# Edge stages of a two-layer graph network: a fixed loop over edge groups, index loads for four groups, row and column tiles on TensorE

## The chip, the core and the metric

The kernel runs as one program on one core of one Trainium2 chip. The metric is the device time of one execution in microseconds (us); lower is better. Engines are called PE (TensorE matmul), PEld (its weight loads), DVE (VectorE), ACT (ScalarE), POOL (GpSimd) and SP (SyncE).

## The reference

There are 12,500 nodes with 128 features and 200,000 edges that are sorted by their destination `dst`. Two message-passing layers run one after the other, each on the layer-normed, clamped nodes, and each is added to the nodes:

```python
# layer 0
h = concat(node[src], node[dst], edge_attr_64) @ W1 + b1
messages = (relu(layernorm(h)) @ W2 + b2) * sigmoid(edge_attr_64 @ gate_w + gate_b)
agg = segment_sum(messages, dst)          # then a GRU cell on agg and the nodes
# layer 1
w = silu(silu(radial(edge_length) @ w0 + b0) @ w1 + b1) @ w2 + b2       # (edges, 4, 32)
m0, m1, m2, m3 = products of w, the sender's features and the edge's direction
out = segment_sum([m0, m3, m1, m2], dst) @ W_out
```

## The kernel before

Edges are worked on in **groups** of 512 (four tiles of 128 edges), 392 groups in all. As the edges are sorted by destination, the destinations of one group nearly always lie in one window of 128 nodes. A group whose destinations spread further gives several items of work, one per window; `node_tables()` writes the list of items into DRAM (`item_group`, `item_base`, `sum_base`), and the number of passes is read from `ctl`. With these inputs no group is that wide, so there are 392 items in 49 passes of eight.

The five stages run one after the other, each with one block per engine:

- `node_tables()` norms the nodes, multiplies them with the two node parts of W1 (`a_table` for senders, `b_table` for receivers, the second in three bf16 parts), prepares the edges' directions and radial embeddings, and makes the list of items.
- `gated_edges()` is layer 0's edge stage. Per group: DVE builds `by_edge` (L769), the one-hot matrix of edges against the window's nodes; PE turns it (L681), ACT copies it (L797); PE multiplies the edge features with a block matrix of two halves, 258 columns (L703), and adds the receivers' rows by 12 bf16 matmuls (L710); DVE adds the senders' rows that POOL gathered (L742); ACT and DVE norm and gate (L810 to L822, L752 to L761); PE sums messages (L690) and gates (L693, the gate's column broadcast to all 128 columns) over the edges; DVE adds the window into `agg` (L778).
- `gru_nodes()` is the GRU cell, and the node part of layer 1 (`u_table`).
- `tensor_edges()` is layer 1's edge stage. Per group PE runs three layers of the radial MLP: L1223, L1229, and L1217 with L1216, where six bf16 matmuls with one row each add the bias. ACT does the two silus (L1258, L1264). POOL gathers the senders' rows (L1192), DVE builds `by_edge` (L1309), makes the messages (L1320 to L1341) and adds the sums into `agg` (L1301); PE sums over the edges (L1238).
- `output_nodes()` multiplies `agg` with the output weights and adds the nodes, which stay in SBUF as `nodes`.

**What sets the order.** In both edge stages the engines are software-pipelined by hand in `step(w, u, drained)`, item `w`, place `u` of eight: PE works on item `w` and `w-1`, the messages lag by 3 or 4 items, the final sum by 6. `over_items()` unrolls the first eight items, loops over the passes and drains. The gathers are four indirect DMAs per group, each issued by POOL from a column of `meta`. Every group has its own small DMAs on SP's queue, which is in order: `meta` (4 KB: sender and destination numbers), `feat` (128 KB) and `b_win` (96 KB) in the gated stage; `meta`, `y` (6 KB) and two of `emb` in the tensor stage; and once per four groups `base`. Before the loads of groups w to w+3 SP waits, in the tensor stage, until DVE has built `by_edge` of group w-5 (`built`, L1165's line is the DMA behind that wait):

```python
if u % BATCH == 0:
    if reached(w, UNROLL):
        sp.wait_ge(built, w - UNROLL + BATCH)
    sp.dma_start(base[:, u:u + BATCH], ...)
if reached(w, UNROLL):
    sp.wait_ge(msg_ready, w - UNROLL + 1)
sp.dma_start(meta[:, u], ...)
```

In the gated stage SP waits before each `b_win` until PE has projected group w-4 (L648), and the next group's `meta` stands behind that. POOL waits for `meta` of its group and for a free buffer of eight:

```python
pool.wait_ge(meta_in[u], 16 * use(w, u) + meta_before)
if reached(w, UNROLL):
    pool.wait_ge(msg_ready, w - UNROLL + 1)
```

## Time and profile before

| what | value |
|---|---|
| runs shown | 6940.47, 6971.14, 6971.62 us; median 6971.14 |
| the profiled execution | 6940.47 us, its span 6939.9 us |
| PE, PEld busy | 68%, 53% of the span |
| DVE, ACT, POOL busy | 45%, 30%, 46% |
| mean granted TensorE clock | 0.781 |
| DMA | 366 MB, 53 GB/s; 507,563 packets, 270,617 of them under 512 bytes |

The span is the time from the first to the last instruction. A busy share is the sum of an engine's recorded instructions; register work, branches, semaphores and the issue of DMAs are not in it, except that POOL's gathers are (their record is the making of descriptors, not the transfer). PE's matmuls overlap, and their ends are modelled. "Idle before" in a row on a group of instructions is the time in which the engine did nothing just ahead of them, with what ended it; "remote" there is an event that the profile can't name. The clock is a share of full speed: 1.00 is the level of 2.4 GHz, 0.50 that of 1.2 GHz.

### The profile page before, as it was taken

Reading aid. Unit: us, or ns where it says so; the run is one execution under the profiler, and the core shown is the slowest. Engines: PE = TensorE matmul, PEld = TensorE weight load, DVE = VectorE, ACT = ScalarE, POOL = GpSimd, SP = SyncE. Lnnn points to the kernel's source line nnn. Section 1 sums busy time; section 2 is a strip of 40 time slices with the busy share of each in tenths; the row PEclk is TensorE's granted clock in tenths of the full one; section 3 lists DMA queues with packets and bytes.
Section 4 is the critical chain, followed back from the end, with each engine's and each line's share of the span. In section 5 each row is a group of like instructions: output and inputs, shape, how many; then the busy total and the mean of one; then the engine's idle time right before and its main releaser. Section 6 shows DMA issues by size and latency. Waiting matters only on the chain. (4 is left out here: it accounts for less than half of the span.)

```text
span 6939.9 us, 102946 instructions
## 1 busy us (share of the span) xinstructions
PE 4728.9 (68%) x27522; PEld 3680.4 (53%) x27522; DVE 3104.2 (45%) x7991; ACT 2052.1 (30%) x7384; POOL 3204.4 (46%) x3226
## 2 busy tenths in 40 slices
PE   5577777777777776778666666666666666666667
PEld 4466566556655665654444444444544455444446
DVE  7444444445444444448343333333343333433334
ACT  5455555545554555543110001000001010100011
POOL 3555555555555555534444444444443444444432
PEclk8787878888887878889777777777777777777778
DMA  6322222223222322221211111111111111111112
GB/s 199 80 70 68 68 67 69 69 67 71 69 67 66 70 68 67 66 53 42 56 31 32 33 32 31 32 33 33 31 32 30 33 33 31 31 31 33 32 30 57
DMA packets 507563, 366.46 MB, mean 53 GB/s; under 512 B 270617, under 2 KB 455842, under 8 KB 507170
## 3 DMA queue, kind: packets, MB, share of 16 engines
q0 software_dynamic: 100496, 208.93, 13.0%
q1 hardware_dynamic: 404002, 146.85, 8.7%
q10 hardware_dynamic: 3026, 10.23, 0.4%
q8 instruction: 15, 0.25, 0.0%
q14 instruction: 24, 0.20, 0.0%
HBM read 327.26 MB, written 38.39 MB: 53 GB/s over the span
## 5 line engine op out<-in xcount | busy, mean ns | idle before, releaser
L1192 POOL DMA_INDIRECT tensor_gath<-u_table,tensor_meta x1568 | 1518.5, 968 | 2060.5 <-DMA tensor_meta<-in_meta 1600.1
L662 POOL DMA_INDIRECT gated_gath<-a_table,gated_meta x1568 | 1538.1, 981 | 1335.7 <-DMA gated_meta<-in_meta 780.5
L1309 DVE SCALAR_TENSOR_TENSOR tensor_by_edge<-iota,tensor_base,tensor_meta 128x512 f32<-128x512 f32 x392 | 294.7, 752 | 2042.5 <-issue 1653.4
L1238 PE MATMUL tensor_agg_ps<-tensor_by_edge,tensor_msg 128*128 128x128 f32 x6272 | 957.0, 301 | 337.2 <-issue 334.8
L1238 PEld LDWEIGHTS tensor_agg_ps<-tensor_by_edge,tensor_msg 128*128 128x128 f32 x6272 | 915.6, 216 | 381.4 <-issue 348.2
L1258 ACT ACTIVATE tensor_h<-tensor_h_ps,tensor_bias 128x256 f32<-128x256 f32 x392 | 186.0, 474 | 3125.4 <-remote 1794.1
L1216 PE MATMUL tensor_w_ps<-tensor_bias_part,tensor_ones 1*128 1x256 bf16 x2352 | 453.9, 306 | 898.8 <-ACT tensor_h L1264 752.1
L742 DVE TENSOR_TENSOR gated_pre<-gated_pre_ps,gated_gath 128x516 f32<-128x516 f32 x392 | 272.0, 694 | 1485.5 <-remote 1246.3
L1216 PEld LDWEIGHTS tensor_w_ps<-tensor_bias_part,tensor_ones 1*128 1x128 bf16 x2352 | 172.2, 99 | 1184.5 <-issue 750.9
L690 PE MATMUL gated_agg_ps<-gated_by_edge,gated_msg 128*128 128x128 f32 x3136 | 572.5, 329 | 218.5 <-issue 129.9
L1217 PE MATMUL tensor_w_ps<-tensor_mlp,tensor_h 128*128 128x256 f32 x1568 | 655.6, 505 | 0.0
L690 PEld LDWEIGHTS gated_agg_ps<-gated_by_edge,gated_msg 128*128 128x128 f32 x3136 | 486.1, 231 | 312.7 <-issue 217.9
L797 ACT CAST gated_by_node<-gated_turned_ps 128x512 bf16<-128x512 f32 x392 | 227.9, 581 | 1272.0 <-remote 987.2
L703 PE MATMUL gated_pre_ps<-gated_w_edge,gated_feat 128*128 128x258 f32 x1568 | 568.8, 444 | 40.1 <-issue 39.5
L710 PE MATMUL gated_pre_ps<-gated_b_win,gated_by_node 128*128 128x128 bf16 x4704 | 470.2, 233 | 177.8 <-issue 176.2
L693 PE MATMUL gated_agg_ps<-gated_by_edge,gated_gate 128*128 128x128 f32 x3136 | 546.5, 323 | 62.5 <-issue 61.0
L710 PEld LDWEIGHTS gated_pre_ps<-gated_b_win,gated_by_node 128*128 128x128 bf16 x4704 | 367.3, 105 | 350.0 <-issue 248.9
L693 PEld LDWEIGHTS gated_agg_ps<-gated_by_edge,gated_gate 128*128 128x128 f32 x3136 | 498.4, 236 | 79.6 <-issue 79.0
L681 PE MATMUL gated_turned_ps<-ident,gated_by_edge 128*128 128x128 f32 x1568 | 295.8, 307 | 340.0 <-DVE gated_by_edge L769 176.4
L810 ACT ACTIVATE gated_junk<-gated_pre 128x128 f32<-128x128 f32 x1568 | 485.8, 310 | 108.7 <-DVE gated_gate L752 46.8
L822 ACT ACTIVATE gated_msg<-gated_msg,gated_gate 128x128 f32<-128x128 f32 x1568 | 494.8, 386 | 0.9 <-DVE gated_msg L761 0.9
L754 DVE SCALAR_TENSOR_TENSOR gated_msg<-gated_pre,gated_rstd,gated_ln_g 128x128 f32<-128x128 f32 x1568 | 444.8, 346 | 0.0
(160 smaller groups left out, 5943.4 us busy)
## 6 DMA issues: line engine op xcount, KB each, us to landing
gated_feat<-in_edge_feat SPq DMA_DIRECT2D x392, 128.0 KB
gated_b_win<-b_table SPq DMA_DIRECT2D x392, 96.0 KB
gated_gath<-a_table,gated_meta POOLq DMA_INDIRECT x1568
tensor_gath<-u_table,tensor_meta POOLq DMA_INDIRECT x1568
tensor_emb<-emb_edges SPq DMA_DIRECT2D x784, 8.0 KB
b_table<-tables_b_out SPq DMA_DIRECT2D x25, 384.0 KB, 3.0
a_table<-tables_a_out SPq DMA_DIRECT2D x25, 258.0 KB, 4.3
tables_x<-in_x SPq DMA_DIRECT2D x25, 256.0 KB, 3.6
```

Of the source, the lines that this page charges most:

```text
L662: nc.gpsimd.indirect_dma_start(gath[:, u, i, :], None, dram["a_table"], bass.IndirectOffsetOnAxis(ap=meta[:, u, i:i + 1], axis=0)).then_in ...
L690: nc.tensor.matmul(agg_ps[v][:, 0:P], msg[:, v, i, :], by_edge[:, z, i, :], start=(i == 0), stop=(i == TILES - 1))
L693: last = nc.tensor.matmul(agg_ps[v][:, P:2 * P], gate[:, v, i:i + 1].broadcast_to([P, P]), by_edge[:, z, i, :], start=(i == 0), stop=(i == ...
L703: nc.tensor.matmul(pre_ps[v][:, t, 0:2 * PRE], feat[:, z, t * P:(t + 1) * P], w_edge[:].rearrange("p h d -> p (h d)"), start=True, stop=False)
L710: last = nc.tensor.matmul(pre_ps[v][:, t, half * PRE:half * PRE + D], by_node[:, v, i * P:(i + 1) * P], b_win[:, z % BATCH, k * D:(k + 1) ...
L754: last = nc.vector.scalar_tensor_tensor(out=msg[:, v, i, :], in0=pre[:, v, i, 0:D], scalar=rstd[:, v, i:i + 1], in1=ln_g[:], op0=ALU.mult, ...
L810: nc.scalar.activation(junk[:], pre[:, v, i, 0:D], ACT.Square, accum_out=ss[:, i:i + 1]).then_inc(squares, 1)
L822: last = nc.scalar.activation(msg[:, v, i, :], msg[:, v, i, :], ACT.Relu, scale=gate[:, v, i:i + 1])
L1192: nc.gpsimd.indirect_dma_start(gath[:, u, i, :], None, dram["u_table"], bass.IndirectOffsetOnAxis(ap=meta[:, u, i:i + 1], axis=0)).then_in ...
L1216: nc.tensor.matmul(out, ones[:], bias2_part[:, k, :], start=(k == 0), stop=False)
L1217: last = nc.tensor.matmul(out, h1[:, v, t * P:(t + 1) * P], mlp2[:], start=False, stop=True)
L1238: last = nc.tensor.matmul(agg_ps[a][:, c * P:(c + 1) * P], msg[:, v, i, MUL + c * P:MUL + (c + 1) * P], by_edge[:, v, i, :], start=(i == 0 ...
```

## The change

- **List.** The loop is fixed: 49 passes over the 392 groups with constants in place of the counters read from `ctl`. What wide groups need beyond their first window is a second list, worked on one item after the other in a short loop behind the first. `ctl[0]` is its length, but at least 1: with these inputs that loop does one empty item per edge stage.
- **Loads.** Sender numbers (`index`), `feat`, `y` and `emb` are loaded for four groups at a time into two halves. `index` of the next half is loaded at places 2 and 6 of a pass, after the gathers that used this half have landed; these waits stand on SP's queue ahead of the `b_win` of places 3 and 7. `b_win` is still loaded per group. Destination numbers of all edges are loaded once (`rel`, 784 KB) and the windows' starts subtracted once; `meta` and `base` are gone, and `by_edge` is one tensor_tensor instead of a scalar_tensor_tensor.
- **PE.** The block matrix of L703 becomes four matmuls of 64 rows and 129 columns per group; L1217 becomes four of 64 rows and 128 columns; the gates' sum (L693) becomes four matmuls of 32 columns side by side, of which the GRU stage takes the sum by a second matmul with `b2` (divided by 32), in place of the DVE operation with a scalar (L1058). The bias of the tensor stage takes two bf16 matmuls per group in place of six.
- **Lags.** In the tensor stage the final sum lags by 5 instead of 6, with two PSUM tiles `agg_ps` instead of four.
- **Nodes.** `nodes` no longer stays in SBUF: `h_table` and `x1_table` in DRAM carry the nodes between stages (25 stores and 25 loads of 256 KB each).

```diff
+                    nc.vector.tensor_scalar(ctl[0:1, 0:1], end_row[0:1, NG - 1:NG], 1.0, None, ALU.max)
...
+                w, h = k * UNROLL + u, u // HALF
                 if u == 0:
-                    loaded["group"] = load_pass(nc, mybir.EngineType.SP, dram["item_group"], w, UNROLL, NG - 1)
-                    loaded["base"] = load_pass(nc, mybir.EngineType.SP, dram["item_base"], w, UNROLL, NP - P)
-                g, first = loaded["group"][u], loaded["base"][u]
-                if u % BATCH == 0:
+                    loaded["first"] = load_bases(nc, mybir.EngineType.SP, dram["group_lo"], w, UNROLL, NP - P)
+                if u % HALF == 0:
                     if reached(w, UNROLL):
-                        sp.wait_ge(by_edge_built, w - UNROLL + BATCH)
-                    sp.dma_start(base[:, u:u + BATCH],
-                                 dram["item_base_f"][0:1, bass.ds(w, BATCH)].broadcast_to([P, BATCH])).then_inc(base_in[u // BATCH], 16)
-                if reached(w, UNROLL):
-                    sp.wait_ge(pre_summed, w - UNROLL + 1)
-                sp.dma_start(meta[:, u], io["meta"][bass.ds(g, 1)].rearrange("a p k -> (a p) k")).then_inc(meta_in[u], 16)
-                sp.dma_start(feat[:, u], io["edge_feat"][bass.ds(g, 1)].rearrange("a p k -> (a p) k")).then_inc(edge_in[u], 16)
-                if reached(w, BATCH):
-                    sp.wait_ge(pre_mm, w - BATCH + 1)
-                sp.dma_start(b_win[:, u % BATCH], dram["b_table"][bass.ds(first, P), :]).then_inc(edge_in[u], 16)
-
-            over_items(sp, step, passes, 0)
+                        sp.wait_ge(pre_mm, w - UNROLL + HALF)
+                    sp.dma_start(feat[:, h].rearrange("p g e -> p (g e)"),
+                                 io["edge_feat"][:, bass.ds(w * (GROUP // 2), HALF * GROUP // 2)]).then_inc(feat_in[h], 16)
+                if reached(w, WINDOWS):
+                    sp.wait_ge(pre_mm, w - WINDOWS + 1)
+                sp.dma_start(b_win[:, u % WINDOWS], dram["b_table"][bass.ds(loaded["first"][u], P), :]).then_inc(window_in[u % WINDOWS], 16)
+                if u == 2:
+
+                    at = sp.snap((w + 2) * TILES)
+                    if reached(k, 1):
+                        for z in range(HALF, UNROLL):
+                            sp.wait_ge(gathered[z], 16 * TILES * k)
+                    sp.dma_start(index[:, 1].rearrange("p g t -> p (g t)"), io["src_tiles"][:, bass.ds(at, HALF * TILES)]).then_inc(index_in[1], 16)
+                if u == 6:
+
+                    at = sp.snap((w + 2) * TILES)
+                    for z in range(HALF):
+                        sp.wait_ge(gathered[z], 16 * TILES * (k + 1))
+                    sp.dma_start(index[:, 0].rearrange("p g t -> p (g t)"), io["src_tiles"][:, bass.ds(at, HALF * TILES)]).then_inc(index_in[0], 16)
+
+            over_items(sp, step, PASSES, 0)
+            sp.wait_ge(index_in[0], 16 * (PASSES + 1))
+
...
+            def step(k, u, drained):
+                w, h = k * UNROLL + u, u // HALF
+                if u % HALF == 0:
+                    pool.wait_ge(index_in[h], 16 * (k + 1))
                 if reached(w, UNROLL):
                     pool.wait_ge(pre_summed, w - UNROLL + 1)
...
+            def aggregate(r, v, z):
+                pe.wait_ge(msg_ready, r + 1)
+                if reached(r, 2):
+                    pe.wait_ge(acc_done, r - 1)
+                for i in range(TILES):
+                    nc.tensor.matmul(agg_ps[v][:, 0:P], msg[:, v, i, :], by_edge[:, z, i, :],
+                                     start=(i == 0), stop=(i == TILES - 1))
+
+                for i in range(TILES):
+                    last = nc.tensor.matmul(agg_ps[v][i * COLS:(i + 1) * COLS, P:2 * P], gate[:, v, i:i + 1].broadcast_to([P, COLS]),
+                                            by_edge[:, z, i, :], start=True, stop=True)
+                last.then_inc(agg_mm, 1)
+
+            def project(r, v, z):
+                if reached(r, 2):
+                    pe.wait_ge(pre_summed, r - 1)
+                edges = feat[:, z // HALF, z % HALF]
+                for t in range(2):
+                    for h in range(2):
+                        rows = slice(h * ED, (h + 1) * ED)
+                        nc.tensor.matmul(pre_ps[v][:, 2 * h + t, 0:PRE], edges[rows, t * P:(t + 1) * P], w_edge[rows, :],
+                                         start=(t == 0), stop=False)
+                pe.wait_ge(by_node_built, r + 1)
+                for i in range(TILES):
+                    for k in range(SPLITS):
+                        last = nc.tensor.matmul(pre_ps[v][:, i, 0:D], by_node[:, v, i * P:(i + 1) * P],
+                                                b_win[:, z % WINDOWS, k * D:(k + 1) * D],
+                                                start=False, stop=(i % 2 == 1 and k == SPLITS - 1))
...
+            dve.wait_ge(dst_in, 32)
+            nc.vector.tensor_tensor(rel[:], rel[:].bitcast(I32), lo_all.unsqueeze(2).broadcast_to([P, NG, TILES]),
+                                    ALU.subtract).then_inc(rel_ready, 1)
...
                     if reached(w, UNROLL):
                         dve.wait_ge(agg_mm, w - UNROLL + 1)
-                    nc.vector.scalar_tensor_tensor(
-                        out=by_edge[:, u], in0=iota[:].unsqueeze(1).broadcast_to([P, TILES, P]), scalar=base[:, u:u + 1],
-                        in1=meta[:, u, TILES:2 * TILES].unsqueeze(2).broadcast_to([P, TILES, P]),
-                        op0=ALU.add, op1=ALU.is_equal).then_inc(by_edge_built, 1)
+                    nc.vector.tensor_tensor(by_edge[:, u], iota[:].unsqueeze(1).broadcast_to([P, TILES, P]),
+                                            rel[:, bass.ds(w, 1), :].rearrange("p g t -> p (g t)").unsqueeze(2).broadcast_to([P, TILES, P]),
+                                            ALU.is_equal).then_inc(by_edge_built, 1)
...
+                    if reached(q, SLOTS):
+                        sp.wait_ge(diff, q - SLOTS + 1)
+                    sp.dma_start(h[:, s], dram["h_table"][bass.ds(q * P, P), :]).then_inc(x_in[s], 16)
+                if has_quad(q - 5, NQ):
+                    r = q - 5
+                    sp.wait_ge(kept, r + 1)
+                    sp.dma_start(dram["x1_table"][bass.ds(r * P, P), :], nodes[:, bass.ds(r * QUAD, QUAD)]).then_inc(x1_stored, 16)
...
-                    nc.tensor.matmul(m_ps[:], w2[:], agg[:, 0, cols], start=True, stop=True).then_inc(m_mm, 1)
+                    nc.tensor.matmul(m_ps[:], w2[:], agg[:, 0, cols], start=True, stop=False)
+                    nc.tensor.matmul(m_ps[:], b2[:], agg[:, 1, cols], start=False, stop=True).then_inc(m_mm, 1)
...
-                    nc.vector.scalar_tensor_tensor(out=mT[:, v], in0=agg[:, 1, bass.ds(q * QUAD, QUAD)], scalar=b2[:, 0:1],
-                                                   in1=m_ps[:], op0=ALU.mult, op1=ALU.add).then_inc(m_copied, 1)
+                    nc.vector.tensor_copy(mT[:, v], m_ps[:]).then_inc(m_copied, 1)
...
-        agg_ps = [pb(f"agg_ps{i}", [P, 512]) for i in range(4)]
+        w_ps = [pb(f"w_ps{i}", [P, TILES, 2 * D]) for i in range(2)]
+        agg_ps = [pb(f"agg_ps{i}", [P, 512]) for i in range(2)]
...
+            def step(k, u, drained):
+                w, h = k * UNROLL + u, u // HALF
+                if u % HALF == 0:
                     if reached(w, UNROLL):
-                        sp.wait_ge(built, w - UNROLL + BATCH)
-                    sp.dma_start(base[:, u:u + BATCH],
-                                 dram["item_base_f"][0:1, bass.ds(w, BATCH)].broadcast_to([P, BATCH])).then_inc(base_in[u // BATCH], 16)
-                if reached(w, UNROLL):
-                    sp.wait_ge(msg_ready, w - UNROLL + 1)
-                sp.dma_start(meta[:, u], io["meta"][bass.ds(g, 1)].rearrange("a p k -> (a p) k")).then_inc(meta_in[u], 16)
-                if isinstance(w, int) and w == 0:
-                    sp.wait_ge(cleared, 1)
-                sp.dma_start(y[:, u].rearrange("p i k -> p (i k)"),
-                             dram["y_edges"][:, bass.ds(g * (TILES * 3), TILES * 3)]).then_inc(edge_in[u], 16)
-                for half in range(2):
-                    sp.dma_start(emb[half * NB:(half + 1) * NB, u],
-                                 dram["emb_edges"][:, bass.ds(g * GROUP + half * HALF, HALF)]).then_inc(edge_in[u], 16)
-
-            over_items(sp, step, passes, 0)
+                        sp.wait_ge(h0_mm, w - UNROLL + HALF)
+                    for part in range(2):
+                        sp.dma_start(emb[part * NB:(part + 1) * NB, h],
+                                     dram["emb_edges"].rearrange("b (g h e) -> h b g e", h=2, e=EDGES)[part, :, bass.ds(w, HALF), :]).then_inc(edges_in[h], 16)
+                    if reached(w, UNROLL):
+                        sp.wait_ge(msg_ready, w - UNROLL + HALF)
+                    sp.dma_start(y[:, h].rearrange("p g t k -> p (g t k)"),
+                                 dram["y_edges"][:, bass.ds(w * (TILES * 3), HALF * TILES * 3)]).then_inc(y_in[h], 16)
+                if u == 2:
+
+                    at = sp.snap((w + 2) * TILES)
+                    if reached(k, 1):
+                        for z in range(HALF, UNROLL):
+                            sp.wait_ge(gathered[z], 16 * TILES * k + GATHERED_BEFORE)
+                    sp.dma_start(index[:, 1].rearrange("p g t -> p (g t)"), io["src_tiles"][:, bass.ds(at, HALF * TILES)]).then_inc(index_in[1], 16)
+                if u == 6:
+
+                    at = sp.snap((w + 2) * TILES)
+                    for z in range(HALF):
+                        sp.wait_ge(gathered[z], 16 * TILES * (k + 1) + GATHERED_BEFORE)
+                    sp.dma_start(index[:, 0].rearrange("p g t -> p (g t)"), io["src_tiles"][:, bass.ds(at, HALF * TILES)]).then_inc(index_in[0], 16)
+
...
+            def layer2(r, v):
+                if reached(r, 2):
+                    pe.wait_ge(msg_ready, r - 1)
+                for h in range(2):
+                    nc.tensor.matmul(w_ps[v][:, 2 * h:2 * h + 2, 0:D], ones[:], bias2_rows[:].rearrange("p (t d) -> p t d", t=2), start=True, stop=False)
+                pe.wait_ge(h1_ready, r + 1)
+                for t in range(2):
+                    for h in range(2):
+                        rows = slice(h * HID, (h + 1) * HID)
+                        last = nc.tensor.matmul(w_ps[v][:, 2 * h + t, 0:D], h1[rows, v, t * P:(t + 1) * P], mlp2[rows, :],
+                                                start=False, stop=(t == 1))
+                last.then_inc(w_mm, 1)
+
+            def aggregate(r, v):
+                pe.wait_ge(msg_ready, r + 1)
+                if reached(r, 2):
+                    pe.wait_ge(acc_done, r - 1)
+                for c in range(2):
+                    for i in range(TILES):
+                        last = nc.tensor.matmul(agg_ps[v][:, c * P:(c + 1) * P],
+                                                msg[:, v, i, MUL + c * P:MUL + (c + 1) * P], by_edge[:, v, i, :],
+                                                start=(i == 0), stop=(i == TILES - 1))
+                last.then_inc(agg_mm, 1)
...
+                if has_quad(q, NQ):
+                    if reached(q, SLOTS):
+                        sp.wait_ge(out_ready, q - SLOTS + 1)
+                    sp.dma_start(x1[:, s], dram["x1_table"][bass.ds(q * P, P), :]).then_inc(x1_in[s], 16)
```

## Rows read from the trace of the kernel before

**Rows 1.** Windows by stage: us, busy us and instructions per engine, granted clock, DMA share, GB/s
```profile
187.00:3060.00 2873.00, 2054.43 (x14034) 1708.51 (x14035) 1372.92 (x3900) 1486.77 (x6241) 1538.09 (x1568) 0.81 0.29 68
3060.00:3322.00 262.00, 213.35 (x830) 123.80 (x829) 182.90 (x500) 90.16 (x160) 84.86 (x51) 0.89 0.18 54
3322.00:6901.00 3579.00, 2336.08 (x11845) 1732.82 (x11846) 1389.17 (x3153) 360.46 (x794) 1518.52 (x1568) 0.75 0.14 32
```

**Rows 2.** Groups of instructions by line: the two gathers on GpSimd
```profile
L662 POOL DMA_INDIRECT gated_gath<-a_table,gated_meta x1568 | 1538.1, 981 | 1335.7 <-DMA gated_meta<-in_meta 780.5 <-issue 455.2 <-DVE gated_pre L742 100.0
L1192 POOL DMA_INDIRECT tensor_gath<-u_table,tensor_meta x1568 | 1518.5, 968 | 2060.5 <-DMA tensor_meta<-in_meta 1600.1 <-issue 460.4
```

**Rows 3.** Waits of the SP queue: us in total, times, longest
```profile
SPq L1165 <- DVE tensor_by_edge L1309: 2007.3, 96, 28.1
```

**Rows 4.** Timeline of GpSimd: end of one train of gathers, start of the next
```profile
5052.89 0.95 POOL L1192 DMA_INDIRECT tensor_gath<-u_table,tensor_meta  x1 [15.78 <-DMA tensor_meta<-in_meta]
...
5072.10 0.95 POOL L1192 DMA_INDIRECT tensor_gath<-u_table,tensor_meta  x1 [0.30 <-issue]
5089.75 0.95 POOL L1192 DMA_INDIRECT tensor_gath<-u_table,tensor_meta  x1 [16.70 <-DMA tensor_meta<-in_meta]
```

**Rows 5.** Windows: one train and gap of the tensor stage, then its first train
```profile
5052.80:5057.80 5.00, 5.00 (x34) 3.94 (x33) 3.18 (x7) 0.91 (x2) 3.99 (x4) 1.00 0.24 50
5057.80:5073.10 15.30, 5.31 (x32) 4.01 (x31) 3.94 (x9) 0.00 (x0) 11.58 (x13) 0.81 0.22 53
5073.10:5089.70 16.60, 12.96 (x60) 9.72 (x60) 7.02 (x16) 2.69 (x6) 0.00 (x0) 0.66 0.03 6
...
3327.80:3363.30 35.50, 12.62 (x32) 6.44 (x30) 5.83 (x13) 2.11 (x5) 26.88 (x29) 0.50 0.24 56
```

**Rows 6.** Timeline of ScalarE over the same train
```profile
5056.26 0.47 ACT L1264 ACTIVATE tensor_h<-tensor_h_ps,tensor_bias 128x256 f32<-128x256 f32 x1
5075.78 0.47 ACT L1258 ACTIVATE tensor_h<-tensor_h_ps,tensor_bias 128x256 f32<-128x256 f32 x1 [19.04 <-remote]
```

**Rows 7.** Windows: one train of eight gathers and its gap in the gated stage
```profile
1505.10:1510.10 5.00, 4.75 (x21) 4.35 (x22) 3.96 (x12) 4.79 (x21) 4.07 (x4) 0.50 0.36 86
1510.10:1515.20 5.10, 4.84 (x43) 4.16 (x43) 0.00 (x0) 0.32 (x2) 3.82 (x5) 0.96 0.23 52
1515.20:1519.50 4.30, 1.47 (x12) 0.78 (x10) 2.95 (x9) 2.53 (x12) 0.00 (x0) 1.00 0.32 81
```

**Rows 8.** Timeline of TensorE: one group of the tensor stage at full clock
```profile
5053.18 0.50 PE L1216 MATMUL tensor_w_ps<-tensor_bias_part,tensor_ones 1*128 1x256 bf16 x3
5053.60 0.70 PE L1217 MATMUL tensor_w_ps<-tensor_mlp,tensor_h 128*128 128x256 f32 x2
...
5057.94 0.28 PE L1216 MATMUL tensor_w_ps<-tensor_bias_part,tensor_ones 1*128 1x256 bf16 x1
```

**Rows 9.** Timeline of TensorE: one group of the gated stage at full clock
```profile
1510.04 0.83 PE L703 MATMUL gated_pre_ps<-gated_w_edge,gated_feat 128*128 128x258 f32 x2
...
1513.21 1.06 PE L693 MATMUL gated_agg_ps<-gated_by_edge,gated_gate 128*128 128x128 f32 x8
1514.11 0.60 PE L703 MATMUL gated_pre_ps<-gated_w_edge,gated_feat 128*128 128x258 f32 x2
```

**Rows 10.** Groups by line: costs near those of the added and removed operations
```profile
L1217 PEld LDWEIGHTS tensor_w_ps<-tensor_mlp,tensor_h 128*128 128x128 f32 x1568 | 275.0, 220 | 205.5 <-issue 205.5
...
L778 DVE TENSOR_TENSOR agg<-agg,gated_agg_ps 128x256 f32 x392 | 162.4, 414 | 4.1 <-PE gated_agg_ps L693 4.1
...
L920 PE MATMUL gru_m_ps<-agg,gru_w 128*128 x32 | 16.4, 594 | 0.0
...
L455 ACT ACTIVATE agg<-agg,tables_centers 128x1568 f32<-128x1568 f32 x8 | 12.8, 1598 | 0.0
```

**Rows 11.** DMA issues by line: KB each, median us to landing
```profile
tensor_meta<-in_meta SPq DMA_DIRECT2D x392, 4.0 KB, 2.1
...
agg<-in_edge_dist ACTq DMA_DIRECT2D x1, 784.0 KB, 4.4
```

798 lines of the change are left out of this document (438 added, 360 removed).

## The prediction

> **What bounds the kernel now.** I read the windows by stage first. The two edge stages take 2873 and 3579 us of the span of 6940, the rest 488 [rows 1]; no engine is busy throughout either (PE 72% and 65%, POOL 54% and 42%). So something alternates. The rows on the gathers say what [rows 2]: POOL's own work, gathers with the 0.3 us ahead of each, is 1538 + 455 = 1993 us in the gated stage and 1519 + 460 = 1979 us in the tensor stage, 5.07 us per group of four gathers. What is left is POOL standing: 880 us (2.25 per group) and 1600 us (4.08 per group), nearly all of it for `meta`. A stage is its gathers plus POOL's standing: 7.33 us per group and 9.13.
>
> In the tensor stage the standing has a fixed form. Sixteen gathers run as one train, 5052.9 to 5073.1, then POOL waits 16.7 us for `meta` [rows 4]. SP issues that only when DVE has built an earlier `by_edge`, and waits for this in total 2007 us [rows 3].
>
> Why is DVE late, with a full-clock PE step of only 4.76 us per group [rows 8]? The windows of one train answer [rows 5]. In its first 5 us DVE does 7 instructions (a group is 8); in the next 15.3 us, 9; PE is busy for 5.3 of those 15.3 and ACT not at all. In the gap the work returns: 16 DVE instructions, two groups. ACT stands for 19.0 us and resumes 2.7 us after the last gather's end [rows 6]. In the stage's first train, which gathers eight groups at a stretch, 35.5 us hold 13 DVE instructions. The gated stage shows the same in a train of eight gathers: DVE 12 instructions in the first half, none in the second, 9 in the gap of 4.3 us [rows 7]. So **while POOL issues gathers without a break, PE and ACT nearly stop after about 5 us, and resume when the train ends.** I don't know the cause; nothing in the program's semaphores asks for it. Its price depends on the length of the trains: 16 gathers and 9.13 us per group in one stage, mostly 4 to 12 and 7.33 in the other.
>
> **The change, part by part.**
>
> *The wait for `meta` goes.* The sender numbers of the next four groups are on chip before they are needed, so POOL is held only by its eight buffers. The gathers cost the same 5.07 us. POOL fills the eight buffers in one long train at the start of each stage and then gets one buffer for each finished group. During a train the others finish about one group in the first 5 us, so the train goes on for a second group and then starves: trains of one or two groups, which is the gated stage's form now. Late next is PE in the gap. For the tensor stage I take the gated stage's period, 7.33 us per group, since the gathers are equal and the full-clock PE steps nearly so (4.07 us from one L703 to the next [rows 9]; 4.76 minus 0.5, below). That is 392 x (7.33 - 9.13) = **-706 us**. Ends: 5.07 per group (-1592) and no gain.
>
> *The gated stage* keeps its form, since its trains are short already. I take **-50 us** for the 100 us of the page's 880 that are not `meta` and for PE's lighter step. Ends: 5.07 per group (-880), and trains as long as the tensor stage's now, 9.13 (+706).
>
> *PE per group.* The two bias matmuls replace six of 0.17 us (0.50 for three [rows 8]): -0.67. L1217 and L703 have the same columns in all and twice the matmuls: 0 if these run one after the other, half of 1.40 and of 1.26 (two of 0.63, near the rows' 0.83 and 0.60 [rows 8, 9]) if two row tiles run together. The gate's matmuls, 1.06 us [rows 9], cost between a quarter and the whole. Against this stands each change of tile shape. The nearest row is the 0.26 us before each of 784 L1217 weight loads that follow bf16 ones [rows 10]; two changes in the tensor stage and four in the gated come to 0.5 and 1.0 us. The trace has no change of tiling to look at. The Trainium skill (TensorEngine Tiling (Array Packing), section Tiling Modes, Key Properties) says that switching the tiling mode drains TensorE, a rule that speaks against this change; it gives no time, and if four drains cost the gated step more than its smaller tiles save, the sum would have +100 to +200 us where it has -50. No row here tests it. I take -0.5 and -0.1 us per group, within the ends -1.4 to +0.5 and -1.4 to +1.0. PE counts only in the gaps, where its step is what ends them, so these are inside the two periods above.
>
> *SP.* Per group 3.25 and 4.25 DMAs become 1.75 and 1. The new waits for landed gathers hold back the `b_win` of places 3 and 7. The cover: PE's projection can be at most two groups ahead of the add of gathered rows, and `b_win` of group 8k+3 is held for the gathers of 8k-1 only. Cost 0; without cover one landing of 2.1 us [rows 11] in 98 half passes, +206. The next `index` is asked for after PE's projection of group w-4 or so, some 1.5 groups later than a buffer is free at the earliest; POOL is then 6.5 groups ahead instead of 8: 0.
>
> *DVE.* `by_edge` drops the scalar operand: 0, DVE waits for PE. Two `agg_ps` instead of four: PE waits for DVE's sum of two groups ago, which now comes one step earlier. Cost 0; without cover 0.41 us [rows 10] x 392 = +163.
>
> *The empty items.* Each edge stage ends with one item in series: a load of 2.1 us [rows 11], four gathers of 5.07, and PE, ACT and DVE one after the other (about 10, two full-clock steps), and the loop's code. **+25 us each**; ends 15 and 60.
>
> *The rest.* The table of destinations is one load like the 784 KB one (4.4 us [rows 11]) and one pass over 1568 elements (1.6 us [rows 10]): **+6**. The GRU stage gets 25 matmuls of 0.594 us [rows 10] on a PE that is busy 213 of 262 us [rows 1]: **+15**. Loads and stores of `h_table` and `x1_table` are prefetched by three or four blocks beside PE: 0, at worst 2.1 us for each of 75, +158.
>
> Sum: 6940 - 706 - 50 + 50 + 6 + 15 = 6255. The profiled execution is the fastest of the three runs, 0.4% under the median of 6971, so I say **6280 us** against the median (-9.9%). Within this case 5850 to 6650, from the ends of PE's step and of the trains' length.
>
> **Rivals.**
>
> *A. The standing still isn't POOL's doing*, but comes from SP's many small DMAs, which start at the same moment. For it: both begin together in every train. Against: in the later 15.3 us of a train SP's loads are over early and PE stands on. Then both stages fall to the gathers: 1993 + 1979 + 488 + 71 = 4531, near **4560 us**. The Trainium skill's page SBUF — State Buffer, section Who interferes with whom, says that DMA never contends with a compute engine, and that PE and ACT never wait on anyone; by that rule this rival is the forecast. The trace here disagrees as far as it can show: ACT's 19.0 us. Chance 0.18.
>
> *B. Gathers and the rest exclude each other whatever the train.* Then the tensor stage's period is 5.07 plus 4.08 as now, and the waits only change name. For it: 5.07 + 4.3 of PE is 9.4, close to 9.13. Against: the gated stage's 7.33. Time 6971 + 71 minus up to 100 for PE: **about 6950**. Chance 0.12.
>
> *C. Longer trains.* POOL is now held by nothing but eight buffers; before, SP's slow issue throttled it. If PE's progress in a train, rather than in the gaps, gives the credit, trains grow to four groups in the gated stage too. The first train of the tensor stage shows what an unthrottled POOL does: eight groups gathered, hardly two worked on [rows 5]. It decides from three groups per train upwards; with half the gated passes at 9.13 the stage gains +353, the tensor stage nothing: 6971 + 353 + 71 = **about 7400 us**. Chance 0.17.
>
> *D. Part of it:* index loads still late, only the tensor stage's 4.5 us from trigger to first gather go, per train: 98 x 4.5 = -441, and with the rest -370: **6600**. Chance 0.08, inside the range.
>
> **How the numbers follow.** The forecast has 0.45. A change under 0.5% (35 us) can't be told from none here. Faster: 0.45 + 0.18 + 0.08 and 0.03 of B, 0.74. Same: 0.07, B's middle. Slower: C and a rest of B, 0.19. The range leaves out C and a little of both ends: 4550 to 7000. It is wide because A lies 1700 us below the forecast; the forecast's own range is the one above.
>
> **What the profile will show.** The POOL row of the tensor gather: wait for `index` near 0, for `msg_ready` or `pre_summed` instead; standing per group 2.2 us instead of 4.1. Trains of 4 to 8 gathers in POOL's timeline, ACT's longest stand under 10 us. PE's L1216 busy time a third. If the gathers are back to back and PE still keeps up, A holds; if the trains have 12 or more and the gated stage is over 3200 us, C.

## The result, and the profile of the changed kernel

The changed kernel takes 6632.98 us (median of 4 runs, 6596 to 6651) where the kernel before takes 6968.77 in the same runs: ratio **0.9516**, 95% interval 0.9481 to 0.9551. It is 4.8% faster; 6280 us had been forecast. The profiled execution has a span of 6625.0 us. There is a second result, in set 4 of the experiments: on another chip the ratio is 1.0176, so the change costs 1.8% there.

Windows of the changed kernel by stage (columns as in [rows 1]), each from the first instruction of its stage:

```profile
0.00:234.50 234.50, 102.09 (x500) 92.92 (x500) 136.10 (x400) 89.31 (x149) 62.59 (x38) 0.69 0.59 190
234.50:3535.70 3301.20, 1959.12 (x15720) 1421.69 (x15720) 1360.96 (x3934) 1485.46 (x6288) 1526.56 (x1572) 0.70 0.24 59
3535.70:3796.10 260.40, 223.31 (x800) 122.12 (x800) 171.82 (x478) 82.65 (x128) 84.64 (x51) 0.91 0.31 100
3796.10:6571.90 2775.80, 1897.16 (x11790) 1582.37 (x11790) 1356.14 (x3159) 356.95 (x788) 1521.32 (x1572) 0.80 0.16 41
```

The windows of [rows 1] don't quite have these edges: at 3060 us the gated stage of the kernel before was still draining (its last matmul ends at 3074.9, and the GRU stage starts at 3080.1). With the same edges the kernel before has:

```profile
184.90:3080.10 2895.20, 2066.77 (x14113) 1720.08 (x14113) 1380.87 (x3925) 1494.25 (x6272) 1538.09 (x1568) 0.81 0.29 68
3080.10:3318.50 238.40, 201.00 (x750) 112.23 (x750) 174.20 (x477) 82.68 (x128) 84.86 (x51) 0.91 0.18 55
3318.50:6887.80 3569.30, 2324.95 (x11760) 1721.69 (x11760) 1385.85 (x3143) 355.64 (x785) 1518.52 (x1568) 0.75 0.14 32
```

The tensor stage got shorter by 793.5 us (3569 to 2776), but the gated stage **got longer by 406** (2895 to 3301), the first stage by 49.6 (184.9 to 234.5) and the GRU stage by 22.0 (238.4 to 260.4); the output stage moved by 1. Together 49.6 + 406.0 + 22.0 - 793.5 + 1.0 = -314.9 us, which is 6939.9 to 6625.0.

Where the gated stage's time went is said by POOL's waits (total, times, longest), which answer to [rows 2]:

```profile
POOL gated_gath L692 <- DMA gated_index<-in_src_tiles: 1239.6, 94, 16.3
POOL tensor_gath L1307 <- DVE tensor_msg L1470: 746.2, 159, 10.6
POOL gated_gath L692 <- DVE gated_pre L789: 23.9, 3, 9.0
```

In the tensor stage the wait for loaded numbers is gone, and POOL waits for a free buffer, as was intended. In the gated stage POOL still waits for a load: 94 times 13.2 us for `index`, where it was 780 us for `meta`. Two times per pass that load comes late, and it then releases four groups at once: in the whole stage 87 trains have exactly 16 gathers. POOL's timeline and SP's, around one of them:

```profile
1005.80 0.94 POOL L692 DMA_INDIRECT gated_gath<-a_table,gated_index  x1 [0.30 <-issue]
1022.95 0.94 POOL L692 DMA_INDIRECT gated_gath<-a_table,gated_index  x1 [16.21 <-DMA gated_index<-in_src_tiles]
```
```profile
1009.79 10.03 SPq L652 DMA_DIRECT2D gated_b_win<-b_table  x3
1020.23 0.33 SPq L665 DMA_DIRECT2D gated_index<-in_src_tiles  x1
```

SP issues `index` (L665) only after three `b_win` (L652), each of which waits until PE has projected a group. POOL starts 2.7 us after the issue and gathers 16 times. The tensor stage asks for `index` at the same places of a pass, but has no `b_win` ahead of it, and there the load isn't late. The tensor stage of the kernel before had this pattern of 16 [rows 4]; now the gated stage has it. Windows of the train that ends at 1006.7, and of the gap behind it:

```profile
990.00:1006.70 16.70, 8.28 (x45) 4.79 (x42) 0.63 (x2) 1.79 (x8) 12.74 (x14) 0.66 0.30 77
1006.70:1022.90 16.20, 11.76 (x95) 9.10 (x96) 10.34 (x31) 10.58 (x46) 0.04 (x1) 0.61 0.09 23
```

DVE does 2 instructions during 16.7 us of train and 31 in the gap of 16.2; ACT stood 17.9 us and resumed 3.0 us after the last gather. That is the reading of [rows 5] again, in another stage.

Two things in it are finer than the prediction has them. First, PE doesn't stop altogether. In the later part of a train it creeps, with one or two matmuls at a time 1.40 us apart, and the profile names nothing that it waits for ("issue"):

```profile
1002.65 0.37 PE L739 MATMUL gated_pre_ps<-gated_w_edge,gated_feat 64*128 64x129 f32 x1 [0.63 <-issue]
1004.05 0.58 PE L739 MATMUL gated_pre_ps<-gated_w_edge,gated_feat 64*128 64x129 f32 x2 [1.03 <-issue]
1005.45 0.37 PE L739 MATMUL gated_pre_ps<-gated_w_edge,gated_feat 64*128 64x129 f32 x1 [0.82 <-issue]
```

Second, the slowing doesn't begin at a fixed 5 us. Here PE slows 4.8 us into the train (987.1 to 991.9). In the train of [rows 5], in the kernel before, it is busy without a gap until 8.5 us into it at least, and only then nearly idle:

```profile
5057.80:5061.40 3.60, 3.60 (x22) 2.54 (x22) 0.42 (x1) 0.00 (x0) 2.68 (x4) 1.00 0.29 62
5061.40:5073.10 11.70, 1.71 (x13) 1.47 (x11) 3.52 (x8) 0.00 (x0) 8.90 (x10) 0.75 0.20 50
```

Of ACT's 19.0 us there, the part up to 5060.6 is an ordinary wait for PE's L1223; the 15.2 us behind it are the stall. The loading of instructions isn't what PE waits for: during 990.0 to 1006.7 two DMA queues move packets, that of the gathers and that of SP's loads, and none of those that carry instructions (40 packets in the whole execution).

```profile
q0 software_dynamic: 448, 0.93, 24.3%
q1 hardware_dynamic: 102, 0.35, 5.2%
```

### The profile page after: what moved, and what is told of

It reads as the page before. It is cut to its first block and busy times, and to the rows that moved or that the text cites. A ratio compares the mean times of both kernels' runs of the same rounds, so it can differ in the third digit from the quotient of the medians.

```text
span 6625.0 us, 100013 instructions
## 1 busy us (share of the span) xinstructions
PE 4229.4 (64%) x29210; PEld 3266.6 (49%) x29210; DVE 3051.0 (46%) x8019; ACT 2029.5 (31%) x7377; POOL 3195.1 (48%) x3233
## 3 DMA queue, kind: packets, MB, share of 16 engines
q0 software_dynamic: 100752, 209.46, 13.2%
## 5 line engine op out<-in xcount | busy, mean ns | idle before, releaser
L692 POOL DMA_INDIRECT gated_gath<-a_table,gated_index x1568 | 1522.8, 971 | 1724.4 <-DMA gated_index<-in_src_tiles 1239.6
L1307 POOL DMA_INDIRECT tensor_gath<-u_table,tensor_index x1568 | 1517.5, 968 | 1246.2 <-DVE tensor_msg L1470 746.2
L1477 DVE TENSOR_TENSOR agg<-agg,tensor_agg_ps 128x256 f32 x393 | 165.2, 420 | 1382.5 <-remote 919.0
L744 PEld LDWEIGHTS gated_pre_ps<-gated_b_win,gated_by_node 128*128 128x128 bf16 x4716 | 329.8, 108 | 658.3 <-issue 625.8
L1346 PE MATMUL tensor_w_ps<-tensor_mlp,tensor_h 64*128 64x128 f32 x3144 | 346.4, 349 | 437.0 <-issue 219.3
L739 PE MATMUL gated_pre_ps<-gated_w_edge,gated_feat 64*128 64x129 f32 x3144 | 429.1, 349 | 189.3 <-issue 185.5
L1346 PEld LDWEIGHTS tensor_w_ps<-tensor_mlp,tensor_h 64*128 64x128 f32 x3144 | 257.2, 229 | 540.6 <-issue 301.0
L871 ACT ACTIVATE gated_junk<-gated_pre 128x128 f32<-128x128 f32 x1572 | 487.1, 310 | 87.5 <-DVE gated_gate L795 44.3
L739 PEld LDWEIGHTS gated_pre_ps<-gated_w_edge,gated_feat 64*128 64x128 f32 x3144 | 307.7, 226 | 322.1 <-issue 320.5
L1341 PE MATMUL tensor_w_ps<-tensor_bias_rows,tensor_ones 128*128 128x256 bf16 x786 | 166.4, 297 | 328.6 <-DVE tensor_msg L1470 324.4
L728 PE MATMUL gated_agg_ps<-gated_by_edge,gated_gate 128*32 128x128 f32 x3144 | 281.2, 327 | 141.1 <-issue 138.6
```

What stands on the lines that cost most here:

```text
L692: nc.gpsimd.indirect_dma_start(gath[:, u, i, :], None, dram["a_table"], bass.IndirectOffsetOnAxis(ap=index[:, h, u % HALF, i:i + 1], axis= ...
L728: last = nc.tensor.matmul(agg_ps[v][i * COLS:(i + 1) * COLS, P:2 * P], gate[:, v, i:i + 1].broadcast_to([P, COLS]), by_edge[:, z, i, :], s ...
L739: nc.tensor.matmul(pre_ps[v][:, 2 * h + t, 0:PRE], edges[rows, t * P:(t + 1) * P], w_edge[rows, :], start=(t == 0), stop=False)
L744: last = nc.tensor.matmul(pre_ps[v][:, i, 0:D], by_node[:, v, i * P:(i + 1) * P], b_win[:, z % WINDOWS, k * D:(k + 1) * D], start=False, s ...
L871: nc.scalar.activation(junk[:], pre[:, v, i, 0:D], ACT.Square, accum_out=ss[:, i:i + 1]).then_inc(squares, 1)
L1307: nc.gpsimd.indirect_dma_start(gath[:, u, i, :], None, dram["u_table"], bass.IndirectOffsetOnAxis(ap=index[:, h, u % HALF, i:i + 1], axis= ...
```

## The experiments

"Per group" is below always (last start minus first start of DVE's write of `by_edge` in the list) / 391; the rows look like these, of the changed kernel, and give 8.32 and 7.01 us (7.33 and 9.10 before the change):

```profile
L828 DVE TENSOR_TENSOR gated_by_edge<-iota,rel x392: 677/684/748, 237.7 to 3490.2; 128x512 f32<-128x512 f32 x196
L1491 DVE TENSOR_TENSOR tensor_by_edge<-iota,rel x392: 678/684/760, 3807.2 to 6546.9; 128x512 f32<-128x512 f32 x196
```

The runs came in five sets, each with the kernel before on the same chip: it took 7076 us in the first, 6975 in the second, 4554 and 4552 in the third and fourth (one and the same chip), 7076 in the fifth. Between sets a difference of a few per cent says little: the gated stage of before_index, which is that of the kernel before, has 7.59 us per group in set 1 for the 7.33 above, and the gated stage of tensor_trains16, which is that of the changed kernel, 8.44 for 8.32. So across sets read nothing into less than some 0.25 us per group.

### Set 1: is it the late index, and is it the gathers at all?

**index_early.** In the gated stage SP asks for both halves of `index` two places earlier:

```diff
-                if u == 2:
-                    at = sp.snap((w + 2) * TILES)
+                if u == 0:
+                    at = sp.snap((w + 4) * TILES)
...
-                if u == 6:
-                    at = sp.snap((w + 2) * TILES)
+                if u == 4:
+                    at = sp.snap((w + 4) * TILES)
```

both ahead of the waits for `feat` and `b_win` of that place.

> The changed kernel; in the gated stage alone SP asks for each half of index two places earlier (places 0 and 4 of a pass, ahead of feat and b_win). Theory T (one late load of index releases 16 gathers at once, and such a train of 16 holds up PE and ACT): POOL's wait for index in the gated stage (1240 us) goes, the trains fall to 4 to 12 gathers, the stage goes from 3300 to 2750 to 2870 us, the whole to 6050 to 6200 us. Rival R1 (the gated stage is slower because PE's row and column tiles cost switches): the wait moves to pre_summed, the stage stays within 100 us of 3300, the whole above 6500. The tensor stage stays at 2787 under both.

Measured: 6069.42 us, ratio **0.8563** (0.8533 to 0.8593). The gated stage takes 2701 us, a little less than T's 2750 to 2870, the tensor stage 2837. POOL's waits:

```profile
POOL tensor_gath L1307 <- DVE tensor_msg L1470: 796.9, 158, 10.2
POOL gated_gath L692 <- DVE gated_pre L789: 618.5, 227, 7.3
```

The wait for `index` has no row any more, and half as much stands for buffers in its place; 145 of the stage's 237 trains have 8 gathers, and only one has more than 11. With two loads asked for earlier the kernel gains 14.4% where the whole change gained 4.8%. T holds; PE's tiles (R1) were not the cause.

**tensor_trains16.** The reverse, in the stage that had gained:

```diff
-                if reached(w, UNROLL):
-                    pool.wait_ge(msg_ready, w - UNROLL + 1)
+                if u % 4 == 0 and reached(w, UNROLL):
+                    pool.wait_ge(msg_ready, w - UNROLL + 4)
```

> The changed kernel; in the tensor stage alone POOL waits at every fourth group until four buffers are free and then gathers four groups (16 gathers) without a wait. Theory T (train length sets the period): the tensor stage goes from 2787 back to 3350 to 3580 us (8.5 to 9.1 per group, as before the change and as the gated stage has now), the whole to 7200 to 7420. Rival R1 (the tensor stage gained because PE has less to do): it stays under 2900, the whole under 6750.

Measured: 7113.6 us; the tensor stage takes 3213 us, 8.13 per group for 7.16 in index_early on the same chip, whose tensor stage is the changed kernel's. The direction is T's and R1's 2900 is excluded, but the size is below T's 3350: trains of 16 cost 1.0 us per group here, not 1.5 to 2.1. What the rest of the kernel before's 9.10 was is not shown; PE's step of 0.96 us less would be about that size, see below.

**before_index.** The kernel before with `index` for four groups in the tensor stage, and nothing else:

```diff
-                pool.wait_ge(meta_in[u], 16 * use(w, u) + meta_before)
+                if u % 4 == 0:
+                    pool.wait_ge(index_in[u // 4], 16 * use(w, u))
```

with the loads of `index` at places 2 and 6, as the change has them.

> The kernel before with one part of the change, in the tensor stage alone: POOL takes the sender numbers from index, loaded four groups at a time two groups ahead, and no longer waits for meta (meta is still loaded for DVE). PE's forms, feat, emb and y stay. Theory T: the tensor stage goes from 3579 to 2780 to 2950 us, the whole to 6150 to 6350; trains of 4 to 12 gathers. Rival R1 (the gain comes from PE's lighter forms): under 150 us gained, the whole above 6800. Rival R4 (SP's many small loads per group hold it up): about half of it, 3100 to 3300.

Measured: 6332.51 us against 7076; the tensor stage goes from 9.10 to 7.28 us per group (7.16 in index_early on the same chip). With PE's old forms and SP's 4.25 DMAs per group this part alone does nearly all that the change does there; the small loads (R4) hardly matter.

**no_gathers.** Loop passes without gathers: DVE adds the rows of the first pass again.

> The changed kernel without the gathers of passes 1 to 48 in both edge stages (and without the loads of index for them): DVE uses the rows gathered in pass 0. All the rest runs. Theory T (PE, ACT and DVE stand because gathers are being issued): with none the stages fall to what PE needs, 4.1 to 5.5 us per group, 1600 to 2150 us each, the whole 3800 to 4900. Rival R3 (the chain PE, ACT, DVE has a period of about 7 us by itself and the gathers only go along): both stages stay above 6.3 us per group, the whole above 5500.

Measured: 4129.86 us; 4.18 and 4.74 us per group. The whole kernel but for the gathers keeps up PE's step in both stages. R3 falls. Its timeline of TensorE also gives the new steps at full clock, from one L1343 (the bias, L1341 of the changed kernel) to the next:

```profile
2987.46 0.38 PE L1343 MATMUL tensor_w_ps<-tensor_bias_rows,tensor_ones 128*128 128x256 bf16 x2
2987.77 0.72 PE L1348 MATMUL tensor_w_ps<-tensor_mlp,tensor_h 64*128 64x128 f32 x8
2988.41 0.70 PE L1331 MATMUL tensor_h_ps<-tensor_emb,tensor_mlp 128*128 128x256 f32 x2
2988.95 0.59 PE L1337 MATMUL tensor_h_ps<-tensor_h,tensor_mlp 128*128 128x256 f32 x2
2989.38 1.95 PE L1358 MATMUL tensor_agg_ps<-tensor_by_edge,tensor_msg 128*128 128x128 f32 x16
2991.26 0.39 PE L1343 MATMUL tensor_w_ps<-tensor_bias_rows,tensor_ones 128*128 128x256 bf16 x2
...
3003.01 0.61 PE L1343 MATMUL tensor_w_ps<-tensor_bias_rows,tensor_ones 128*128 128x256 bf16 x2 [4.15 <-DVE tensor_msg L1472]
```

The step is 3.80 us where it was 4.76 [rows 8]. The four row tiles (L1348) take 0.72 us for 1.40: **two row tiles do run together**. Once per pass PE waits some 4 us for DVE (4.15 above), and the group behind that runs at the lower level, with a granted clock of 0.51, and takes 6.8 us instead of 3.8; the two together make the mean 4.74. The gated step:

```profile
1001.81 1.16 PE L725 MATMUL gated_agg_ps<-gated_by_edge,gated_msg 128*128 128x128 f32 x8 [0.36 <-ACT gated_msg L884]
1002.90 0.42 PE L729 MATMUL gated_agg_ps<-gated_by_edge,gated_gate 128*32 128x128 f32 x8
1003.25 0.72 PE L740 MATMUL gated_pre_ps<-gated_w_edge,gated_feat 64*128 64x129 f32 x8
1003.90 0.84 PE L745 MATMUL gated_pre_ps<-gated_b_win,gated_by_node 128*128 128x128 bf16 x12
1004.58 0.61 PE L717 MATMUL gated_turned_ps<-ident,gated_by_edge 128*128 128x128 f32 x4
1005.62 1.16 PE L725 MATMUL gated_agg_ps<-gated_by_edge,gated_msg 128*128 128x128 f32 x8 [0.43 <-ACT gated_msg L884]
```

3.81 us for 4.07 [rows 9]: the gates' sum takes 0.42 for 1.06, the block matrix 0.72 for 1.26. Across the three changes of tiling (L725 to L729 to L740 to L745) each group of matmuls begins before the one ahead of it has ended by the profile, so no drain shows there. Of the Trainium skill's rule that a change of tiling mode drains TensorE (TensorEngine Tiling (Array Packing), section Tiling Modes, Key Properties) no cost is visible here, though those ends are modelled; what is measured is that the step got shorter by 0.26 us with these changes in it.

### Set 2: what in a gather holds the others up?

Three kernels leave out or replace part of the gathers in `index_early`, one takes away the wait of the first stage.

> index_early with two of the four gathers of each group in passes 1 to 48 left out, in both edge stages. Four gathers cost 2.60 us per group in the gated stage (6.83 against 4.23 without) and 2.41 in the tensor stage (7.17 against 4.76). Theory P (what the gathers cost is proportional to the time in which they are being issued): 5.5 and 6.0 us per group, the whole 5000 to 5200. Theory W (the others get a part in every train, so short trains cost nothing): 4.3 to 4.6 and 4.8 to 5.1, the whole 4200 to 4450.

Measured: 4308.53 us; 4.62 and 4.78 us per group. Half of the gathers cost 0.43 and 0.04 us per group, the other half 2.2 and 2.4 (2.0 and 2.2 against h_stored, which ran on the same chip and has 6.65 and 6.98). P falls. W fits, but 371 of the gated stage's 387 trains have two gathers, and the median gap between trains is 2.0 us: the run doesn't tell a short train from a long silence behind it.

> index_early with four gathers per group, but each of 64 rows instead of 128 in passes 1 to 48 (half of the rows are left out), in both edge stages. Theory I (POOL's issuing as such holds the others up) and a gather's time on POOL unchanged near 0.98 us: 6.8 and 7.1 us per group, the whole 6000 to 6100. Theory D (the rows in flight, their descriptors and transfers, hold them up): half of 2.60 and 2.41 go, 5.5 and 6.0 us per group, the whole 5000 to 5200. If a gather's time on POOL halves as well, the run doesn't tell the two apart.

Measured: 6047.71 us; 6.70 and 7.15 us per group, no less than h_stored's 6.65 and 6.98 on the same chip, with a gather still 0.92 to 0.98 us on POOL. The gathers' queue, in index_early and here:

```profile
q0 software_dynamic: 100752, 209.46, 14.8%
q0 software_dynamic: 100752, 108.40, 8.5%
```

The bytes fell by half, the number of packets didn't. This excludes that half of D which says that the bytes moved hold the others up. It leaves the other half, the number of packets and whatever POOL writes for each, as well as I.

> index_early with, in the tensor stage alone, the gathers of passes 1 to 48 replaced by four memsets of 128x1100 f32 on POOL, each about 1 us (the gathered rows are those of pass 0). Theory I (POOL being busy, whatever with, holds the others up): the stage stays near 7.1 us per group. Theory D (it takes gathers): 4.8 to 5.3 us per group, the stage 1900 to 2100 us instead of 2830. The gated stage stays at 6.8 under both.

Measured: 5132.05 us; the tensor stage has 4.71 us per group with POOL this busy:

```profile
L1314 POOL MEMSET tensor_busy<- 128x1100 f32 x1536 | 1559.6, 1015 | 317.0 <-POOLq L1316 176.4 <-POOLq L1307 138.3 <-DVE tensor_msg L1477 1.9
```

As many instructions of the same length as gathers, at about the same density, cost nothing against 4.74 in no_gathers. So POOL's being busy (I) isn't the cause: it takes gathers, which is what D says in this run. Together with half_rows, what is left is something that every gather does whatever its bytes: its issue on POOL, or its 32 packets. These two weren't told apart.

**h_stored.** The store of `hT` gets semaphores of its own (and four others are merged):

```diff
-                    sp.dma_start(dram["h_table"][bass.ds(r * P, P), :], hT[:, z]).then_inc(stored[z], 16)
+                    sp.dma_start(dram["h_table"][bass.ds(r * P, P), :], hT[:, z]).then_inc(h_stored[z], 16)
...
-                        act.wait_ge(stored[z], 48 * (quad_use(r, z) - 1))
+                        act.wait_ge(h_stored[z], 16 * (quad_use(r, z) - 1))
```

> index_early, and in node_tables() the stores of hT count on semaphores of their own, so that ACT's write of hT waits for the store of hT alone and not for the stores of a_out and b_out of the same slot (four other semaphores are merged to make room). If that wait (86.5 us in the changed kernel) is what lengthened the first stage from 187 to 234 us, the stage falls to 190 to 200 us and the whole by 30 to 45 us against index_early (ratio to before 0.850 to 0.853 for 0.856). Rival: the DMA traffic of the stores itself did it; then it stays within 10 us.

Measured: 5927.18 us, ratio **0.8502** (0.8473 to 0.8532); the first stage ends at 194.1 us for 237.6 in index_early (and for 235.3, 235.0 and 239.2 in the three other kernels of this set, which don't have the edit). ACT's write of `hT` in the changed kernel, and in h_stored:

```profile
L438 ACT ACTIVATE tables_hT<-tables_hT_ps 128x512 f32<-128x512 f32 x25 | 14.9, 597 | 97.5 <-DMA b_table<-tables_b_out 86.5 <-PE tables_hT_ps L522 11.0
```
```profile
L440 ACT ACTIVATE tables_hT<-tables_hT_ps 128x512 f32<-128x512 f32 x25 | 14.8, 593 | 48.8 <-PE tables_hT_ps L524 48.8
```

The wait on the store of `b_out`, which came with the shared semaphore, is what lengthened the stage. Beside that the traffic of the stores and all else that was added to the stage cost 9 us at most (184.9 to 194.1, on two chips).

### Set 3: pauses, and a chip on which nobody stands

> h_stored with a pause of POOL after every second gather in passes 1 to 48 of both edge stages (a memset of 128x400 f32 and a wait for its end, some 0.5 us), so that gathers come in twos 0.8 us apart; POOL's own work is then about 6.1 us per group. Theory S (a train of two gathers holds nobody up, as two_gathers seems to say, and a short pause ends a train): POOL sets the period, 6.1 to 6.3 us per group in both stages where h_stored has 6.70 and 6.98, the whole 5350 to 5600 us, ratio 0.77 to 0.80. Theory L (what two_gathers had was not the shortness of its trains but the 2.4 us of silence behind each; half a us ends nothing): no better than h_stored, 6.7 to 7.6 us per group, the whole 5900 to 6400.

Measured: 6247.87 us, ratio 1.3713 (1.369 to 1.3736), since the kernel before took **4553.78 us** here (7 runs, 4552 to 4560).

> h_stored with one pause of POOL of about 0.9 us (memset of 128x800 f32 and a wait for it) behind the four gathers of each group, in both edge stages; POOL's own work about 5.9 us per group, no train longer than four. Theory S: 5.9 to 6.3 us per group, the whole 5300 to 5600. Theory L: 6.6 to 7.4, the whole 5850 to 6200.

Measured: 5925.22 us. Both times lie in L's ranges, but they say nothing on S and L, since POOL's own work alone explains them. POOL's timeline of fours:

```profile
1499.06 0.95 POOL L695 DMA_INDIRECT gated_gath<-a_table,gated_index  x1 [0.30 <-issue]
1500.01 0.78 POOL L699 MEMSET gated_pause<- 128x800 f32 x1
1501.78 0.95 POOL L695 DMA_INDIRECT gated_gath<-a_table,gated_index  x1 [0.98 <-POOLq L693]
```

Behind the memset POOL stands 0.98 us, for the wait and the increments, where it stands 0.30 between gathers. A pause is thus 0.78 + 0.68 us here, and POOL alone needs 4 x (0.99 + 0.30) + 1.46 = 6.6 us per group; in pairs it is 7.2, with two pauses of 1.05. That is what was measured (6.67 and 6.93; 7.18 and 7.25). Whether short pauses help where the stall exists is open.

> index_early with three of the four gathers per group in passes 1 to 48, in both edge stages: POOL's issuing is 3.8 us per group, between 2.5 (two_gathers: 4.66 and 4.79 us per group) and 5.1 (index_early: 6.83 and 7.17). A cost proportional to the gathers beyond two: 5.6 to 5.9 and 5.9 to 6.1, the whole 5000 to 5250. A cost that needs POOL to issue without gaps: with 1 us or more of POOL's time free per group 4.8 to 5.2 in both, the whole 4450 to 4650.

Measured: 4089.29 us, 4.14 and 4.69 us per group, less than with two gathers in set 2. More gathers in less time can't be explained by the kernel, nor can the kernel before at 4554.

> index_early with the gated stage's sum over the gates (L728) as before the change: four matmuls of 128 columns that add up, instead of four of 32 columns side by side. At full clock it costs PE 0.64 us more per group (1.06 against 0.42). Theory: PE's step counts only while POOL is silent, so the stage gets 0.1 to 0.4 us per group slower, 40 to 160 us. Rival (switches of the column tiling cost more than they save): it gets faster. Rival (PE off the path altogether): within 20 us.

Measured: 4658.73 us, where index_early had 6069. (The sum of the gates comes out four times as large in it, as `b2` keeps its scale; the matmuls are those of the kernel before.) POOL gathers 1568 times without a gap, 5.16 us per group in the gated stage. So the question became the chip.

### Set 4: the changed kernel itself on that chip

> The changed kernel, unaltered, once more. On the chip of the last four runs the kernel before took 4554 us where it takes 6940 to 7100 elsewhere, and gates_wide gathered without a break at 5.2 us per group in both edge stages. Theory C (there are chips on which gathers don't hold up the others): on such a chip the changed kernel takes 4600 to 4700 us, 1 to 3% more than the kernel before, since the stages are gathers there and the first stage got longer; on one of the others 6600 to 6750, ratio 0.945 to 0.955. Rival (the 4554 us had to do with what else ran then): the kernel before takes 6940 to 7100 on every chip from now on and the ratio is near 0.95.

Measured: the kernel before 4552.25 us, the changed kernel **4632.15** (4631 to 4638): ratio **1.0176**, 95% interval 1.0158 to 1.0194. Theory C holds. Stage by stage, with the same edges as above (the first stage ends at 235.3):

```profile
235.30:2281.20 2045.90, 1499.17 (x15720) 1166.78 (x15720) 1372.00 (x3935) 1491.81 (x6288) 1529.11 (x1572) 0.93 0.39 96
2281.20:2541.60 260.40, 223.35 (x800) 122.11 (x800) 171.73 (x479) 82.69 (x128) 84.74 (x51) 0.91 0.30 99
2541.60:4578.20 2036.60, 1624.19 (x11790) 1371.83 (x11790) 1364.94 (x3158) 359.55 (x788) 1529.48 (x1572) 0.92 0.23 56
```

Same program: the first and the GRU stage take what they took on the first chip (235.3 for 234.5, and 260.4 us), POOL's gathers last as long (1529 us for 1572 of them), and the edge stages are 1255 and 739 us shorter. PE no longer stands, and its granted clock is 0.93 and 0.92 for 0.70 and 0.80. ACT's copies of `by_node` follow each other at the gathers' own pace, in the midst of a train of 1568, where the first chip had stands of 18 us:

```profile
1004.67 0.56 ACT L859 CAST gated_by_node<-gated_turned_ps 128x512 bf16<-128x512 f32 x1
1010.33 0.56 ACT L859 CAST gated_by_node<-gated_turned_ps 128x512 bf16<-128x512 f32 x1
1015.48 0.59 ACT L859 CAST gated_by_node<-gated_turned_ps 128x512 bf16<-128x512 f32 x1
```

The change costs 80 us here. Its own additions, by the traces of the first chip, are 108: 50 us of the first stage, 22 of the GRU stage, 1 of the output stage and the two empty items (16 and 19 us, below). The other 28 us are not accounted for, since no trace of the kernel before was taken on this chip. That it too is gathers from end to end there, so that the rest of the change can gain little, is argued from its time alone.

> h_stored, unaltered, beside it. Theory C: on a chip without the hold-up 4560 to 4640 us, 40 to 45 us less than the changed kernel, as only the first stage differs where POOL gathers without a break; on one of the others 5900 to 6050, ratio 0.85.

Measured: 4611.50 us, 20.6 less than the changed kernel instead of 40 to 45: the first stage gives 41 us, but a gather of the gated stage is at 986 ns for 973 and takes 20 of them back.

### Set 5: the two kernels of set 3 where the stall exists

> three_gathers once more (index_early with three of four gathers per group in passes 1 to 48), for a chip with the stall; on the chip without it it took 4089 us, 4.18 and 4.71 us per group. With the stall, a cost proportional to the gathers beyond two: 5.6 to 5.9 and 5.9 to 6.1 us per group, the whole 5000 to 5250. A cost that needs POOL to issue without gaps: 4.8 to 5.2 in both, the whole 4450 to 4650. If this is the chip without the stall, 4080 to 4100.

Measured: 4985.53 us; 5.43 and 5.70 us per group. Above the 4.18 and 4.74 of none, the gathers cost 0.43 and 0.04 for two, 1.25 and 0.95 for three, 2.60 and 2.42 for four (the four runs are of three chips). The cost grows with each gather beyond the second, and by more for the fourth than for the third; both forms expected were a little off, the first (beyond two, in proportion) is the nearer. The same kernel needs 896 us less on the chip without the stall.

> gates_wide once more (index_early with the gates' sum in four matmuls of 128 columns), for a chip with the stall. Theory (PE's step counts only while POOL is silent): the gated stage 0.1 to 0.4 us per group slower than index_early's 6.83, 40 to 160 us. Rival (column tiling costs more than it saves): faster. If this is the chip without the stall, 4655 to 4665, where the stage is gathers and PE's step costs nothing.

Measured: 6085.60 us, ratio 0.8594 (0.8566 to 0.8622); the gated stage has 6.85 us per group for 6.78, and the intervals of the two ratios overlap. The tensor stage, which is the same in both kernels, has 7.10 for 7.16, so 0.06 is what two chips differ by. 0.64 us of PE per group (L728 with 128x128 weights in place of 32 columns) come to at most 0.07 us, and no effect is shown. PE is all but off the path when the trains are short; column tiles cost the stage nothing that shows, and bring it nothing either.

## Why the prediction was right and wrong

**The cause was right, on the chips that have it.** That PE, ACT and DVE are held up during a train of gathers, and that its price grows with the train, is shown by four runs: no_gathers (4.18 and 4.74), two_gathers, index_early, tensor_trains16. What it is in a gather that does so remains open. "After about 5 us" was the edge of a window and not a reading: PE worked on for 8.5 us in that train, and in [rows 7] it is busy for 4.84 us of the 5.10 in which it was said to be nearly stopped; there only ACT and DVE stand.

**The tensor stage: -706 forecast, -793.5 measured**, which has an empty item in it; 7.01 us per group for the 7.33 taken over from the gated stage. The wait on buffers is as said. POOL stands 1.9 us per group (7.01 - 5.07), where 2.2 was named. The trains are longer than the 4 to 8 gathers forecast: 72 of 4, 46 of 8 and 66 of 12. ACT's longest stand inside the passes is 16.9 us and not under 10, though 37 stands over 10 us are left of 96. before_index shows that the index did it.

**The gated stage: -50 forecast, +406 measured. This is the step that failed.** The prediction had seen the delay: "The next `index` is asked for after PE's projection of group w-4 or so, some 1.5 groups later than a buffer is free at the earliest; POOL is then 6.5 groups ahead instead of 8: 0." It put a smaller lead at 0 and forgot what a load for four groups does to the pattern. When such a load lands that late, the buffers of three of its four groups are free (so it is in each of the 87 trains of 16), the fourth comes free during the train, and POOL gathers 16 times at a stretch: it stands 1240 us for `index`, and a group takes 8.32 us. index_early, which takes the delay away, brings the stage to 6.78. The upper end given for this stage, 9.13 us per group for trains "as long as the tensor stage's now", named what happened, but the sum didn't use it. The sum of 6255 against the profiled execution becomes, term by term: +456 for this stage, -87.5 for the tensor stage, -50 for the empty items (they are inside the two stages as measured), +43.6 for the first stage, +7 for the GRU stage, +1 for the output: 6625.1, which is the span of 6625.0.

**Luck in the numbers.** 6633 us lies inside the range of 5850 to 6650, at its upper edge, but not by the reasons given for the range: the error of +456 is larger than what the range allowed above 6280, and what else came out lower, 87.5 us in the tensor stage above all, brought the sum back to the range's edge. Rival D's 6600 is nearer than the forecast, and by luck too: it has the late load in the tensor stage, where 441 us were to be gained and 793.5 were, and knows nothing of the loss in the gated stage.

**PE.** The terms were too small and hardly mattered. The steps at full clock fell by 0.96 and 0.26 us, where 0.5 and 0.1 were taken. With short trains little of it counts: the tensor stage has 7.28 us per group with the old forms and 7.16 with the new on the same chip, 0.12 of 0.96, and gates_wide_again at most 0.07 of 0.64. With trains of 16 the period is 8.13 for 9.10, about the whole 0.96, but on two chips and with other loads beside it, so that this is argued. A slip without weight: SP's DMAs per group in the gated stage become 1.5 (`b_win`, a quarter each of `feat` and `index`), not 1.75.

**The first stage: +6 forecast (for the table of destinations), +49.6 measured.** Loads and stores of `h_table` and `x1_table` were put at 0, at worst +158. The worst case covers it, the 0 was wrong: the added store counts on a semaphore that it shares, and ACT then waits for the latest of three stores. h_stored shows that this is some 40 us of it.

**Small terms.** An empty item costs 16 and 19 us, not 25: from the last build of `by_edge` in the list to the end of PE's last matmul over it 39.3 and 24.1 us after, 23.0 and 5.4 before. The 25 matmuls of the GRU stage were put at 15 us; the stage got longer by 22.0. The start of one block's `m_ps` to that of the next, before and after:

```profile
3142.45 1.02 PE L920 MATMUL gru_m_ps<-agg,gru_w 128*128 x2
3148.90 1.02 PE L920 MATMUL gru_m_ps<-agg,gru_w 128*128 x2
```
```profile
3600.61 1.02 PE L1009 MATMUL gru_m_ps<-agg,gru_w 128*128 x2
3607.91 1.02 PE L1009 MATMUL gru_m_ps<-agg,gru_w 128*128 x2
```

6.45 us become 7.30. PE has no room there, and one such matmul is two records (x2) that take 0.85 us of its step together, where the prediction took 0.594, the length of one record; 25 x 0.85 = 21 us.

**The rivals.** C named the place and its sign (the gated stage above 3200 us, trains above 12) but another cause, a POOL held by nothing; in the tensor stage, where POOL is held by nothing but buffers, the trains have 4 to 12 gathers. Its 7400 had no tensor gain in it. A gave 4560 us, and there is a chip with 4552 and 4632, though for a reason that A did not have: there the kernel before has that time as well. The Trainium skill's rule that DMA never contends with a compute engine and that PE and ACT wait on nobody (SBUF — State Buffer, section Who interferes with whom) agrees with that chip's trace, and half_rows agrees in that the bytes moved cost nothing; on the other chips ACT's 17.9 us and PE's steps of 1.40 us, which no semaphore of the program explains, speak against it. B (the waits only change name) is excluded by the tensor stage's 7.01 us per group for 9.10; its own argument set 4.3 us of PE, which is the step after the change (4.76 - 0.5), against a time from before it, when the step was 4.76.

## What to carry to other kernels

When several small loads become one larger one, ask not only whether it comes in time but what it lets go at once when it is late: a queue that was throttled in steps of one now moves in steps of four. Place the request by the consumer's earliest need, ahead of in-order waits that belong to other buffers, and look in the profile for the new load among the releasers of the engine that it feeds. A new store on an existing semaphore makes every waiter of that semaphore wait for it, so give it its own. When stages of two profiles are compared, cut both at the same event. And repeat the comparison on more than one chip when an engine stands for no reason that the program has.

## What was not expected of the hardware

- Chips differ. The kernel before takes 6940 to 7104 us in the first runs and in sets 1, 2 and 5, and 4546 to 4560 us in sets 3 and 4, which ran on one chip, each within 1% from run to run on one chip; the changed kernel 6596 to 6651 and 4631 to 4638. The difference lies in the stretches with indirect DMAs on GpSimd alone. It is laid to the chip because both sets on that chip show it and the sets around them don't; whether that chip always does so wasn't tried.
- Where the stall exists it needs gathers on POOL, and grows from the third per group on (with two per group it costs 0.43 and 0.04 us). Memsets of the same length don't cause it, and halving the bytes of each gather, with as many packets, changes nothing. ACT and DVE stand, PE creeps with one or two matmuls each 1.40 us. What they wait for is in no row of the profile ("remote", "issue"), and remains open, as does how long a silence ends it, and what is different in the chip.
- Row tiles: four matmuls of 64 rows take 0.72 us for the 1.40 us of two of 128 rows [rows 8], both at full clock; in the gated stage it is 0.72 for 1.26, the prediction's figure.

The best version on the chips with the stall is h_stored, 15.0% faster than the kernel before (index_early 14.4%, the change 4.8%). On the chip without it the kernel before is the fastest of those tried, with h_stored at 1.0127 (1.0105 to 1.0149).
